# Cross attention: key, value and output projections placed at other head steps

## The reference

```
Q = layernorm(x) Wq' + bq ; K = ctx Wk' + bk ; V = ctx Wv' + bv      (16 heads of 16)
A = softmax(mask(Q K' / 4)) V ;  x1 = x + tanh(g_xattn) * (A Wo' + bo)
```

## Time and profile before

| what | value |
|---|---|
| median of three runs | 1934.24 us |
| the profiled execution | 1932.07 us, span 1930.3 us |
| TensorE matmul, weight load | 97%, 59% of the span |
| VectorE, ScalarE, GpSimd | 76%, 59%, 49% of the span |
| stretch 300 to 400 us: matmul, weight load, VectorE, ScalarE, GpSimd | 99.81, 84.00, 86.50, 86.92, 24.36 us |
| the same stretch: granted TensorE clock, DMA share | 1.00, 0.82 |
| the chain of waits that ended last | names nothing in this stage |

### The profile page before, as it was taken

The page is one execution under the profiler, slowest core; times in us unless marked ns, Lnnn a source line. Parts: engine busy times, 40 slices in busy tenths (PEclk is TensorE's granted clock), DMA queues, the critical chain, the costliest instruction groups (busy, mean ns, idle before and its releaser), DMA issues. The chain is left out here.

```text
span 1930.3 us, 57615 instructions
## 1 busy us (share of the span) xinstructions
PE 1871.1 (97%) x13454; PEld 1145.8 (59%) x13454; DVE 1476.6 (76%) x4245; ACT 1135.5 (59%) x3591; POOL 951.1 (49%) x1432
## 2 busy tenths in 40 slices
PE   5899999999997999999999999999999999999998
PEld 3688888888875555444444445545555555555543
DVE  6688888888887961555555556658999999999989
ACT  3688888888886444444444445545555555555543
POOL 4022222222212001666666666666677676776766
PEclk9999999999998999999999999999999999999999
DMA  6677888788862484000000023122222222222201
GB/s 156 122 118 117 120 119 120 118 120 119 120 88 88 202 329 188 27 27 27 14 27 27 27 82 97 50 71 66 71 80 67 79 75 72 79 70 76 75 15 64
DMA packets 192148, 174.22 MB, mean 90 GB/s; under 512 B 51921, under 2 KB 183378, under 8 KB 190034
## 3 DMA queue, kind: packets, MB, share of 16 engines
q1 hardware_dynamic: 189906, 165.06, 37.7%
q0 software_dynamic: 2176, 8.39, 1.2%
HBM read 112.41 MB, written 60.98 MB: 90 GB/s over the span
## 5 line engine op out<-in xcount | busy, mean ns | idle before, releaser
L1496 POOL TENSOR_TENSOR o_side<-o_side,o_tmp 128x256 f32 (+1 forms) x528 | 397.2, 752 | 195.8 <-POOL o_side L1496 72.8
L1265 PE MATMUL e_pv<-e_vw,e_xhi 128*128 (+1 forms) x1600 | 475.9, 379 | 1.2 <-ACT e_out L1188 1.2
L1198 ACT ACTIVATE big<-e_pv,gates 128x128 f32<-128x128 f32 x800 | 227.9, 368 | 280.8 <-PE e_pv L1265 279.3
L1624 ACT ACTIVATE o_tmp<-o_py,gates 128x256 f32<-128x256 f32 x528 | 221.8, 473 | 193.0 <-PE o_py L1696 143.8
L661 ACT ACTIVATE c_ex<-c_sm,c_nmax 100x361 f32<-100x361 f32 x512 | 302.1, 592 | 53.5 <-DVE c_nmax L554 46.2
L554 DVE CUSTOM_DVE_ANT_0 c_sm<-c_ps,c_mbias 100x361 f32<-100x361 f32 x512 | 267.4, 523 | 55.9 <-PE c_ps L746 51.2
L1696 PE MATMUL o_py<-o_whi,a_chi 128*128 128x512 f16 x800 | 304.2, 380 | 0.1
L1696 PE MATMUL o_py<-o_wlo,a_chi 128*128 128x512 f16 x800 | 303.8, 380 | 0.0
L1696 PE MATMUL o_py<-o_whi,a_clo 128*128 128x512 f16 x800 | 303.7, 380 | 0.0
L1265 PE MATMUL e_pv<-e_vw,e_xlo 128*128 (+1 forms) x800 | 303.2, 379 | 0.0
L1131 DVE TENSOR_SCALAR e_acc<-e_pv,gates 128x128 f32<-128x128 f32 x400 | 121.8, 346 | 227.5 <-PE e_pv L1265 227.4
(11 more groups left out here) (164 smaller groups left out, 3206.4 us busy)
## 6 DMA issues: line engine op xcount, KB each, us to landing
qk<-e_out SPq DMA_DIRECT2D x16, 1600.0 KB, 5.2
c_kst<-k_parts SPq DMA_DIRECT2D x256, 90.2 KB, 4.9
a_q<-qk SPq DMA_DIRECT2D x64, 200.0 KB, 2.4
a_k<-qk SPq DMA_DIRECT2D x64, 200.0 KB, 2.4
v<-e_out SPq DMA_DIRECT2D x20, 640.0 KB, 3.3
a_v<-v SPq DMA_DIRECT2D x64, 200.0 KB
c_ctx<-in_ctx_t SPq DMA_DIRECT2D x32, 361.0 KB, 3.4
e_wst<-in_v_w POOLq DMA_DIRECT2D x8, 1024.0 KB, 7.7
```

The lines of the kernel that those rows point to most:

```text
L1198: act.activation(tmp[:, hh, e, :], p_v[:, hh, 1, e * PD:(e + 1) * PD], ACT.Copy, scale=gate).then_inc(s_av, 1)
L1265: last = pe.matmul(p_v[:, hh, half, :], a[:, c, bass.ds(t * P, P)], vw[:, bass.ds(col + (w * DC + c) * VW, 512)], start=j == 0, stop=j == ...
L1496: pool.tensor_tensor(side[:, x.t, :], side[:, x.t, :], tmp[:, slot(x, r), j, :], ALU.add).then_inc(s_pool, 1)
L1624: act.activation(tmp[:, slot(x, r), j, :], p_y[:, q, j, :], ACT.Copy, scale=gate).then_inc(s_av, 1)
```

## The change

The keys of b+2 come first in a batch (steps 1, 2, 3, 5), then the values of b+1 (6, 7, 9, 10, 11, 13), and the projection is cut in its two halves, in steps 14 and 15 (11 and 12 in the last batch). `key_hi` and `key_lo` stand in steps 3 and 5, the copies of the values in steps 8, 11 and 14. The reading of the turned reciprocals moves from step 6 to 7, the normalization from 7 to 9. `residual`, mean and variance follow one batch later, in steps 0, 1 and 2, and so do the store and `keep`. The lag between scores and turning is the same.

```diff
@@ SP
                 if later(b, 3):
                     load_ctx(later(b, 3))
+                if has_two_before(b):
+                    store(b.before().before())
                 if later(b, 2):
                     stack_keys(later(b, 2))
-                if not is_first(b):
-                    store(b.before())
@@ GpSimd
-                if not is_first(b):
-                    keep(b.before())
+                if has_two_before(b):
+                    keep(b.before().before())
@@ VectorE
-                    if i == 15 and later(b, 2):
-                        key_lo(later(b, 2), 0)
-                    if i == 0 and not is_first(b) and later(b, 1):
-                        key_lo(later(b, 1), 1)
+                    if i in (3, 5) and later(b, 2):
+                        key_lo(later(b, 2), i // 5)
                     if i == 2 and not is_first(b):
                         invert(b.before())
-                    if i == 7 and not is_first(b):
+                    if i == 9 and not is_first(b):
                         normalize(b.before())
-                    if i == 11 and not is_first(b):
-                        residual(b.before())
-                    if i == 12 and not is_first(b):
-                        moments(b.before())
-                    if i == 13 and not is_first(b):
-                        mean_var(b.before())
+                    if has_two_before(b):
+                        tail(b.before().before(), i)
+                    if is_last(b):
+                        tail(b.before(), i - 12)
@@ ScalarE
-                    if i == 15 and later(b, 2):
-                        key_hi(later(b, 2), 0)
-                    if i == 0 and not is_first(b) and later(b, 1):
-                        key_hi(later(b, 1), 1)
-                    if i == 6 and not is_first(b):
+                    if i in (3, 5) and later(b, 2):
+                        key_hi(later(b, 2), i // 5)
+                    if i == 7 and not is_first(b):
                         copy_rt(b.before())
-                    if i == 4 and not is_last(b):
-                        values(b.next(), 0)
+                    if i in (8, 11, 14) and not is_last(b):
+                        values(b.next(), (8, 11, 14).index(i))
                     exp(b, i)
-                    if i in (6, 9) and not is_last(b):
-                        values(b.next(), (4, 6, 9).index(i))
@@ TensorE, keys
-                    at_least(pe, s_vz, KC * b.n - c)
+                    done = b.n if isinstance(b.n, int) and b.n < 2 else b.n - 1
+                    at_least(pe, s_vz, KC * done - c)
@@ TensorE, values
+                    elif is_last(b):
+                        pe.wait_ge(s_vz, KC * b.n)
                     else:
-                        pe.wait_ge(s_klo, DC * b.n + c + 1)
+                        keyed = b.n if is_first(b) else b.n + 1
+                        pe.wait_ge(s_klo, DC * keyed + c + 1)
@@ TensorE, order
-            ahead = {1: (1, values, 0, 0), 2: (1, values, 0, 1), 3: (1, values, 1, 0), 5: (1, values, 1, 1),
-                     7: (1, values, 2, 0), 9: (1, values, 2, 1),
-                     11: (2, keys, 0, 0), 13: (2, keys, 0, 1), 14: (2, keys, 1, 0), 15: (2, keys, 1, 1)}
-            behind = {5: (turn_rden,), 10: (project_all,)}
+            ahead = {1: (2, keys, 0, 0), 2: (2, keys, 0, 1), 3: (2, keys, 1, 0), 5: (2, keys, 1, 1),
+                     6: (1, values, 0, 0), 7: (1, values, 0, 1), 9: (1, values, 1, 0), 10: (1, values, 1, 1), 11: (1, values, 2, 0), 13: (1, values, 2, 1)}
+            behind = {5: (turn_rden,), 14: (project, 0), 15: (project, 1)}
+            behind_last = {5: (turn_rden,), 11: (project, 0), 12: (project, 1)}
```

More of the change, by code:

```diff
@@ L97, in is_last, with has_two_before @@
     return isinstance(b.n, int) and b.n == NB - 1
+def has_two_before(b):
+    return not isinstance(b.n, int) or b.n >= 2
 def later(b, n):
@@ L468, in rest @@
                 batches(sp, body)
+                store(fixed(NB - 2))
                 store(fixed(NB - 1))
@@ L528, in gpsimd @@
             spread(fixed(NB - 1))
+            keep(fixed(NB - 2))
             keep(fixed(NB - 1))
@@ L606, in start, with tail @@
                                       ALU.mult).then_inc(s_tg, 1)
+            def tail(b, step):
+                if step == 0:
+                    residual(b)
+                if step == 1:
+                    moments(b)
+                if step == 2:
+                    mean_var(b)
             def body(b):
@@ L795, in project @@
                     last.then_inc(s_o, 1)
-            def project_all(b):
-                for c in range(DC):
-                    project(b, c)
             def start(n):
@@ L830, in body @@
                         work(later(b, n), *args)
-                    if i in behind and not is_first(b):
-                        work, *args = behind[i]
+                    owed = behind_last if is_last(b) else behind
+                    if i in owed and not is_first(b):
+                        work, *args = owed[i]
                         work(b.before(), *args)
```

## The result

| kernel | median (range), runs | ratio to before, 95% interval |
|---|---|---|
| before | 1934.14 us (1933.02 to 1935.41), 5 | |
| changed | 1943.60 us (1941.63 to 1946.12), 5 | 1.005 [1.0035, 1.0065] |

The change makes the kernel 0.5% slower: +9.5 us, where +12 was forecast. The profiled execution of the changed kernel takes 1943.6 us (span 1941.8), 11.5 more than that of before.

The account below looks back on a forecast made before the run. TensorE was taken to bound the stage with 95% of the time, a VectorE-ScalarE chain the other 5%. 1932.07 + 14 - 2.8 + 0.5 = 1943.8, with 2.2 for the median 1946 us; range 1938 to 1955, 8 in 10 1922 to 1957.

Parts of the forecast that it names:

- The step that decides: Step 5: `key_hi`(1) waits behind exp(4), which needs a late masking; starts at 6.25, free at 6.83 us.
- The walk: Engine queues followed through one batch: 1.14 us lost before step 8's scores, 0.23 in step 8; 16.6 us per batch.
- The period: Time of one batch: 16.6 us forecast against 16.1 before, +0.5 us per batch.
- The loads: SP's key and query loads come earlier, so waits for queries and mask go: -2.8 us, bounds 1.3 and 3.5.
- +14 - 2.8 + 0.5: Forecast sum: longer batches over 28 counted batches, load waits gone, late context in batch 1.
- Batch 0: Has keys computed ahead but little beside them, so left out of the 28 batches counted at +0.5 us.
- batches 30 and 31: Last two batches, without keys; VectorE bounds their light steps before and after: zero, within 1 us.
- The +0.5 for a late context in batch 1: Batch 1's context comes late from the prologue: some +0.5 us.
- The split: GpSimd's context split ready at 17.4, needed at 17.9: half a microsecond slack, zero cost; rival of a late split 8%.
- The projection in two halves: TensorE's 1.32 and 0.46 us steps become two of 0.89, equal in sum: zero.
- the waits of TensorE go: Rival, 20%: even filling removes TensorE's waits, faster; decided by `key_hi`(1) starting by 6.1 instead of 6.83 us.
- 1918 for half and 1905 for all of the waits: Times in us if half or all of TensorE's waits vanish; all gone is -29 us.

Follow-up runs that it names:

- `half_queries`: Kernel before with four of a batch's eight query loads left out, same instructions on every engine but SP; 1926.12 us, ratio 0.9966.
- `hi1_ahead`: Changed kernel with ScalarE's rounding of key block 1 ahead of the exponentials of head 4 instead of behind them; 1917.45 us, 0.9928 of before.

## Why the prediction was right

- *The step that decides* was right in place and size: `key_hi`(1) behind exp(4) behind masking 4 behind `key_lo`(0). Seven starts of the chain agree within 0.08 us, and cutting it at either end took most of the wait in step 7 away (0.2 to 0.3 of 1.00 us left). The walk gave 1.14 + 0.23 us; the trace shows 1.00 in step 7 and 0.33 in step 8. Its total, 1.37 against 1.33, is right; the share of step 8 was short by 0.1, because attend matmuls behind a late turning start 0.49 instead of 0.39 us after it (see the end).
- *The period* came out as 16.6 to 16.7, forecast 16.6.
- *The loads*: direction right, size too small. I took 2.8 us with an upper bound of 3.5, since the earlier trace rows name only waits that the trace put down to the load. Leaving half of the loads out gave 6. The waits in step 15 of a third of the batches were in the trace but are not put down to a load there (the one ahead of the scores at 407.44 in the kernel before is put down to VectorE's masking); a table of all steps over all batches would have shown them. In the same way I compared with 16.07 as the period of before, which is that of a batch without a late load; the mean from batch 2 to 29 is 455.1 / 28 = 16.25. Without late loads (`half_queries`) it is 450.9 / 28 = 16.10; the changed kernel's is 467.0 / 28 = 16.68, so the chain costs 16 us in these batches, not 14. That the total came out close is in part luck, since the two errors offset each other: +14 - 2.8 + 0.5 = +11.7 forecast, +16 - 6 = +10 measured by parts. Two more terms were off and cancel. Batch 0, which I took to have little beside its keys, takes 1.3 us more than before (15.66 against 14.35), for its steps 5 and 7 are 1.83 and 1.81; batches 30 and 31, put at zero, take 1.2 less together. The +0.5 for a late context in batch 1 did not come: its step 1 takes 0.95, as in every batch.
- *The split* had slack, as in the walk: 0.7 us, where the walk gave 0.5.
- *The projection in two halves* I priced at zero, its sum being the same. TensorE's rows bear the price out: steps 14 and 15 take 0.89 each. Against the changed order without it, though, this part is worth 19 us. I missed that moving the keys away from steps 14 and 15 leaves them nearly empty and that the projection fills them: the price of one part depends on the other. How much of the 19 us is the filling and how much the later place of `residual` and the statistics stays open.
- *The rivals*: "the waits of TensorE go" was not what happened, but its condition was the right one: the rounding of block 1 by 6.1 us. With it at 6.04 (`hi1_ahead`) steps 7 and 8 lose 0.5 us together, where I had 0.4, and the time is 1917; with both `key_lo` spaced it is 1903. I had 1918 for half and 1905 for all of the waits. The Trainium skill (Perfetto Trace Analysis, Identifying Performance Opportunities) says that improving a kernel generally means improving its most-contended engine. By that sentence alone the kernels would all be equal; the measurement decides otherwise: ten kernels with the same TensorE instructions, in three orders, span 1903 to 1962 us, and those in the changed order alone 1903 to 1944.

## What to carry to other kernels

When two engines pass a piece of work to a third in turn, don't put both halves in the same step: the second engine idles for the first one's queue, and if the next piece's first half stands behind work that the idle engine feeds, the delays chain. Give the second half a step or more of distance. And look at the length of each step over all batches, not only at what the waits are put down to: steps shorter than the slowest helper's share of work are paid later, and a load that is late now and then hides in a step that is short most of the time.

## What the runs showed of the hardware

Three transposes that start after a wait take 0.56 us instead of 0.46 in these rows, and the attend matmuls behind them start 0.49 instead of 0.39 us later. So a wait of 0.23 us costs 0.33 at that place (step 8 of the kernel before and after). The rows of the weight loads of the kernel before show where the 0.1 us goes:

```profile
302.22 0.39 PEld L753 LDWEIGHTS c_pt<-ident,c_ex 100*121 100x121 f32 x3 [0.26 <-DVE c_ext L564]
...
306.42 0.45 PEld L753 LDWEIGHTS c_pt<-ident,c_ex 100*121 100x121 f32 x3
```
